# A two-layer block on one core: bodies of the mixer written out for all batches, with the jobs of all five engines in another order

## The reference

```python
h = _layernorm(x) * (1 + ca) + sa
# linear attention, 16 heads of 16
qf, kf = elu(h @ wq.T) + 1, elu(h @ wk.T) + 1
kv = einsum('bhsd,bhse->bhde', kf, h @ wv.T)
x = x + ga * ((qf @ kv) / (qf . sum(kf) + EPS) @ wo.T + bo)
h = _layernorm(x) * (1 + cb) + sb
# softmax attention, 16 query heads, 4 key and value heads, 512 x 512 scores for each head
scores = einsum('bhqd,bhkd->bhqk', q, k) / sqrt(16)
src = h + softmax(scores) @ v @ ow + ob
src = _rmsnorm(src, norm1_w)
src = src + _moe(src, gate_w, w1, w2)     # sigmoid router, top 2 of 8 experts, capacity
x = x + gb * _rmsnorm(src, norm2_w)
```

## Time and profile before

| engine | busy us | share of the span | instructions |
|---|---|---|---|
| PE | 3107.1 | 92% | 18289 |
| DVE | 2105.6 | 63% | 5860 |
| ACT | 1634.8 | 49% | 3647 |
| POOL | 1203.8 | 36% | 1507 |

### The profile page before, as it was taken

How to read it: one execution, slowest core, us unless ns; L and a number is a source line. 1 busy time by engine, 2 the same in 40 slices (tenths; PEclk the granted TensorE clock), 3 DMA queues, 4 the chain that set the end, 5 groups by cost and what they waited for, 6 DMA issues and landing times. The chain is left out here.

```text
span 3365.7 us, 58089 instructions
## 1 busy us (share of the span) xinstructions
PE 3107.1 (92%) x18289; PEld 1914.7 (57%) x18289; DVE 2105.6 (63%) x5860; ACT 1634.8 (49%) x3647; POOL 1203.8 (36%) x1507
## 2 busy tenths in 40 slices
PE   6899999999989977999999999999999859999995
PEld 3667767677665653344444444444444338888882
DVE  7777777777772235677777777777777632222225
ACT  3565565655641113666666666666666521111113
POOL 2132232322342123334444444444443234444445
PEclk9999999999999988999999999999999979999998
DMA  8010100101025851112222222222222128888866
GB/s 265 5 48 24 41 30 24 47 24 40 32 70 195 300 187 35 51 54 72 74 74 74 74 69 73 72 72 68 73 69 75 52 75 216 215 219 217 219 187 200
DMA packets 269091, 337.44 MB, mean 100 GB/s; under 512 B 43679, under 2 KB 218386, under 8 KB 268832
## 3 DMA queue, kind: packets, MB, share of 16 engines
q1 hardware_dynamic: 239840, 296.62, 28.3%
q0 software_dynamic: 28464, 34.71, 4.8%
q10 hardware_dynamic: 544, 3.15, 0.2%
HBM read 225.77 MB, written 113.95 MB: 101 GB/s over the span
## 5 line engine op out<-in xcount | busy, mean ns | idle before, releaser
L2426 ACT ACTIVATE pT<-psum 128x512 f32<-128x512 f32 x1024 | 599.2, 599 | 362.5 <-PE psum L3204 343.6
L2720 DVE TENSOR_REDUCE negmax<-psum 128x2 f32<-128x1024 f32 x512 | 624.6, 1221 | 199.1 <-PE psum L3174 182.0
L3204 PE MATMUL psum<-q_stack,k_stack 99*128 99x512 bf16 x1024 | 379.3, 384 | 20.8 <-issue 10.5
L3174 PE MATMUL psum<-k_stack,q_stack 96*128 96x512 bf16 x1024 | 312.2, 387 | 47.0 <-DVE negmax L2720 37.3
L3535 POOL DMA_INDIRECT src_rows<-ye,place x142 | 222.7, 1568 | 317.3 <-DVE place L3571 140.1
L939 ACT ACTIVATE probs<-probs,negmax 128x256 f32<-128x256 f32 x512 | 252.8, 495 | 137.7 <-DVE negmax L1031 134.0
L3548 ACT ACTIVATE actT_x<-psum 128x512 f32<-128x512 f32 x142 | 84.8, 597 | 439.6 <-PE psum L3624 429.4
L3587 DVE TENSOR_SCALAR ye<-psum,weight 128x256 f32<-128x256 f32 x142 | 62.2, 480 | 361.4 <-PE psum L3636 361.3
L3218 PE MATMUL psum<-pT,v_tile 128*32 128x512 f32 x2048 | 275.0, 609 | 1.0 <-ACT pT L2426 1.0
L3624 PE MATMUL psum<-xT_x,w_x 128*128 128x256 f32 x1136 | 258.5, 381 | 0.0
L3636 PE MATMUL psum<-w_x,actT_x 128*128 128x256 f32 x1136 | 256.6, 379 | 0.0
(11 more groups left out here) (392 smaller groups left out, 5805.3 us busy)
## 6 DMA issues: line engine op xcount, KB each, us to landing
w_x<-in_L_ffn_w_dram SPq DMA_DIRECT2D x142, 512.0 KB, 4.6
w_e<-in_L_ffn_w_dram SPq DMA_DIRECT2D x46, 1024.0 KB, 6.8
q_stacks<-q_part SPq DMA_DIRECT2D x192, 128.0 KB
q_stack<-q_stacks SPq DMA_DIRECT2D x64, 384.0 KB, 3.6
padded<-w_e SPq DMA_DIRECT2D x32, 650.0 KB, 6.0
xe<-padded SPq DMA_DIRECT2D x71, 260.0 KB
gate_rows<-mods SPq DMA_DIRECT2D x66, 256.0 KB, 3.4
x<-in_L_attn_x_dram SPq DMA_DIRECT2D x16, 512.0 KB, 8.7
```

Of the source, the lines that this page charges most:

```text
L2426: act.activation(pT[:, 4 * (s % 2) + r, :], bank(m, 2 + n % 2), ACT.Exp, scale=float(DHQ) ** -0.5)\
L2720: dve.tensor_reduce(negmax[:, p // 2, h:h + 2], m.psum[:, at:at + 2, :], AX.X, ALU.max, negate=True)\
L3174: mm = pe.matmul(bank(m, at + j), q_stack[0:K_SCORE, h, t * P:(t + 1) * P], k_stack[0:K_SCORE, g, :], start=True, stop=True)
L3204: pe.matmul(bank(m, 2 + n % 2), k_stack[:, g, kc * P:(kc + 1) * P], q_stack[:, REP * g + r, :], start=True, stop=True).then_inc(sT_done, 1)
```

## The change

The job functions stay as they are, but for one thing: the three Newton steps on VectorE get scratch tiles of their own, which lets two of them stand next to each other. The bodies lose their loop over steps, the hardware loop goes, and every engine has its jobs written out in another order. Body -1 becomes `entry()`, with the same jobs in the same order. Every job of every batch is there as often as before. The line numbers of the jobs on TensorE grow by 144, those on GpSimd by 2.

```diff
-            for b in range(-3, 2):
+            for b in range(-3, -1):
                 body(b, b % 2, lambda k: 0 <= b + k < B)
-            with loop(nc, pe, 0, 2) as i:
-                for u in range(4):
-                    body(4 * i + (u + 2), u % 2, lambda k: True)
-            for b in range(10, B + 3):
+            entry()
+            for b in range(0, B + 3):
                 body(b, b % 2, lambda k: 0 <= b + k < B)
...
-            def newton(step, out, var, eps, last):
-                h = m.newton[:, 0:NT]
+            def newton(step, h, out, var, eps, last):
...
-                newton(step, rstd1[:, :], mv1[:, :, 1], LN_EPS, stats1)
+                newton(step, m.newton[:, 0:NT], rstd1[:, :], mv1[:, :, 1], LN_EPS, stats1)
...
-                newton(step, rstd2[:, par, :], mv2[:, par, :, 1], LN_EPS, rstd2_ready)
+                newton(step, m.newton[:, NT:2 * NT], rstd2[:, par, :], mv2[:, par, :, 1], LN_EPS, rstd2_ready)
...
-                newton(step, rstdr[:, :], mvr[:, :, 1], EPS_NORM, rstdr_ready)
+                newton(step, m.var_eps[:, 0:NT], rstdr[:, :], mvr[:, :, 1], EPS_NORM, rstdr_ready)
```

```diff
                     max_rows(b + 1, 0)
-                if part(1):
-                    load_h2_rows(b + 1)
-                if part(1):
-                    store_second(b + 1)
-                if part(3):
-                    load_rows(b + 3)
-                if part(1):
-                    load_stack(b + 1, 2)
-                if part(-1):
-                    store_src(b - 1, 1 - par)
-                if part(1):
-                    load_stack(b + 1, 3)
-                if part(1):
-                    max_rows(b + 1, 1)
+                    store_second(b + 1)
+                    load_stack(b + 1, 2)
+                    load_stack(b + 1, 3)
+                    max_rows(b + 1, 1)
+                if part(-1):
+                    store_src(b - 1, 1 - par)
+                if part(1):
+                    load_h2_rows(b + 1)
+                if part(3):
+                    load_rows(b + 3)
```

VectorE and ScalarE, one place each of the new bodies (ScalarE's `second_part(b + 1, 2)` stood at step 13, between two `exps` of that step):

```diff
+                if part(1):
+                    row_max(b + 1, 1, 0)
+                if part(-1):
+                    choose_top(b - 1)
+                if part(1):
+                    row_max(b + 1, 1, 1)
+                    row_max(b + 1, 1, 2)
+                if part(2):
+                    gate(b + 2, 0)
+                if part(-1):
+                    choose_index(b - 1)
+                if part(1):
+                    row_max(b + 1, 1, 3)
...
+                if part(1):
+                    copy_max(b + 1, 0)
+                if part(2):
+                    copy_o1T(b + 2, 1)
+                if part(1):
+                    second_part(b + 1, 2)
```

More of the change, by code:

```diff
@@ L3413, in _ @@
-            for b in range(-3, 2):
+                if part(0):
+                    scoresT(b, 0, 0)
+                if is_entry(b - 1):
+                    project1(1, 0)
+                    project1(1, 1)
+                if part(0):
+                    max_scores(b, 1, 4)
+                    scoresT(b, 0, 1)
+                if part(2):
+                    transpose_hidden(b + 2, 0)
+                if part(0):
+                    scoresT(b, 0, 2)
+                if part(-1):
+                    weigh(b - 1, 15, 1 - par)
@@ new lines, in body @@
+                if part(1):
+                    transpose_hidden2(b + 1, 1)
+                if part(0):
+                    weigh(b, 3, par)
+                    max_scores(b, 2, 4)
+                if part(-1):
+                    transpose_weighed(b - 1, 3)
+                if part(1):
+                    queries_keys(b + 1, 0)
+                if part(0):
+                    max_scores(b, 2, 5)
+                    scoresT(b, 4, 2)
+                    scoresT(b, 4, 3)
+                if part(2):
+                    keys_values(b + 2, 1)
@@ new lines, in body @@
+                if part(2):
+                    keys_values(b + 2, 3)
+                if part(0):
+                    scoresT(b, 9, 2)
+                    max_scores(b, 3, 7)
+                    scoresT(b, 9, 3)
+                    weigh(b, 8, par)
+                    scoresT(b, 10, 0)
+                if part(1):
+                    max_scores(b + 1, 0, 0)
+                if part(0):
+                    scoresT(b, 10, 1)
+                    weigh(b, 9, par)
+                    transpose_max(b, 3)
+                    scoresT(b, 10, 2)
@@ new lines, in body @@
+                if part(0):
+                    scoresT(b, 15, 0)
+                if part(1):
+                    max_scores(b + 1, 1, 1)
+                if part(0):
+                    scoresT(b, 15, 1)
+                if part(2):
+                    project1(b + 2, 0)
+                if part(1):
+                    max_scores(b + 1, 1, 2)
+                if part(0):
+                    scoresT(b, 15, 2)
+                    scoresT(b, 15, 3)
+                if part(1):
+                    values(b + 1)
@@ L3414, in _ @@
+                if part(0):
+                    weigh(b, 14, par)
+                if part(1):
+                    max_scores(b + 1, 1, 3)
+                if part(2):
+                    project1(b + 2, 1)
+            for b in range(-3, -1):
                 body(b, b % 2, lambda k: 0 <= b + k < B)
-            with loop(nc, pe, 0, 2) as i:
-                for u in range(4):
-                    body(4 * i + (u + 2), u % 2, lambda k: True)
-            for b in range(10, B + 3):
+            entry()
```

934 lines of the change are left out of this document (577 added, 357 removed).

## The result

The changed kernel takes 3394.22 us (median of 4 runs, 3387.26 to 3410.70), beside 3367.11 for the kernel before. The ratio is 1.0084, with a 95% interval of 1.0066 to 1.0102: 0.8% slower, where 1% faster was forecast. The profiled execution of the changed kernel took 3387.26 us, the shortest of the four; its span is 3385.5.

What follows compares the result with a forecast made beforehand. TensorE (PE), 95% busy, was taken to bound the mixer, so only its standing time could be won: -1.3 - 0.4 - 0.7 - 0.5 + 0.5 - 0.3 = -2.7 us a body, 13 bodies, -35 us: 3333 us, range 3305 to 3371.

Steps and rivals of the forecast that it cites:

- GpSimd and SyncE: `last_part(b + 1, 2)` ends 2 to 3 us later, but `store_second` does not move; costed at nothing.
- rival 3: Slower: GpSimd's chain ends 6 us later than forecast, TensorE waits 4 us a body; +17, 3385 us; chance 0.11.
- the same sum: `cut_max(b + 1, 0)` and `choose_top` lie under GpSimd's resid work instead of its xn work, at the same price.
- Place A: First pairs of the next batch: 1.98 us of waits go, 0.3 left, 0.4 new stack-transfer wait; 1.3 us less a body.
- rival 1: Transfers decide Place A: it gives 0.3 us instead of 1.3; -22, 3346 us; chance 0.20.
- Place B: End of the body: 1.0 us goes, 0.2 stays, 0.4 new at pair (1, 4) of the next; 0.4 us less.
- Places C and D: Behind `keys_values(b + 2, 2)`, 0.7 us less a body; at `queries_keys(b + 1, 0)`, 0.5 us less.
- Elsewhere: New waits at `max_scores(b, 3, 1)`, (3, 5) and `project2(b - 1, 1)`: +0.5 us a body; small old waits go: -0.3.
- The loop: Writing out bodies 2 to 9 is worth 0 to 6 us, mostly counted in place C already; taken as 0.
- Rival 2: The waits only move and VectorE keeps bodies at 87 us: 3368 us, at most 5 either way; chance 0.14.

Runs made afterwards that it cites:

- the kernel of 3326.8: The changed kernel with GpSimd's whole body in the order of before and `place(b - 2)` in its early spot on VectorE: 3326.82 us, ratio 0.9894.
- the kernel with both moves undone: The changed kernel with `place(b - 2)` back early on VectorE, `add_bias` and `normalise_first` back on GpSimd: 3349.85 us, ratio 0.9949.
- the mirror: The kernel before, loop and other engines' orders kept, with GpSimd's body alone in the changed order: 3415.72 us, ratio 1.0150.

## Why the prediction was wrong, step by step

**The step that failed** is the one on GpSimd and SyncE, "so nothing moves ... I cost this at nothing". It looked at GpSimd's new order only for when its own results are ready (rival 3), and not for what VectorE does meanwhile. It should have read +35 us (with `place` early) to +57.5 us (with it late), over 13 bodies 2.7 to 4.4 us each. Neither `place`, moved from behind (b, 2, 5) to behind (b, 3, 0), nor `scale_src` has a term in the forecast at all, though in the old trace GpSimd was idle beside both: at `place` in a wait of 26.85 us that ScalarE's q_part ended, at `scale_src` in its wait for src ("4.09 <-DVE src L2793"). That idle time was the cover, and the change filled it. What the runs showed in place of the nothing: `over` and the copy longer by 3.4 us a body together, `scale_src` by 3.1, and PE's waits behind them of 2.9 to 3.1 and 1.9 us.

**The rule was cited and then confined.** The Trainium skill ("SBUF — State Buffer", Who interferes with whom) says that a VectorE instruction with two SBUF inputs contends with a GpSimd instruction that reads SBUF, that a copy, cast or tensor_scalar in a two-port mode and a GpSimd instruction block each other fully, that the order of issue decides who blocks, and that `tensor_reduce` never contends. By that rule, the traces agree: 166 to 2393 ns for the copy, 478 to 1249 for `scale_src`, 1221 to 1219 for the reduction. The forecast applied it to `cut_max` and `choose_top` alone and concluded "the same sum". Each of the other moved jobs had to be held against GpSimd's new neighbours.

**What held.** In a body of the changed kernel (body 8) PE's waits of 0.15 us or more are: 0.44, 2.87, 0.23, 0.37 and 1.88. Without the two large ones that is 1.04, where body 8 of before has 3.35.
- Place A: the wait of 0.63 is gone, the second stays, 0.37 for 0.39; no wait for a k_stack DMA appears, so the 0.4 taken for it was wrong, and rival 1 with it.
- Place B: the 0.82 is gone, and a new wait of 0.44 stands exactly at (b + 1, 1, 4), behind `choose_index` and the reduction of (1, 3); 0.4 was taken.
- Places C and D: the third product waits no more (0.59 before), nor does `queries_keys` (0.36). The 0.44 of the prediction was a mean with one wait of 1.51 in it.
- Elsewhere: 0.5 was added for three new waits. In body 1, which nothing hides, PE has only two waits of 0.15 us or more, 0.44 at place B and 0.23 at (b + 1, 0, 4); none of the three named is there.
- The sum of these, -2.7 us a body, fits where nothing hides it: body 1 fell by 3.3 us, and the kernel of 3326.8 lies 31.8 below the one that is only written out, for 35 forecast. That difference has the same GpSimd order on both sides.
- The loop: 0 was taken, 0 to 6 allowed, 7.8 measured. "Most of that difference is place C" was wrong: written out without a job moved, place C's wait stays, and only its excess in looped bodies goes.

**Of the rivals**, the third had the sign and its engine, and even its price (3385 for 3394), but not its mechanism: it named GpSimd held up by VectorE and late stacks, and it was VectorE held up by GpSimd, with no wait for a stack. That its price came so near is luck. Rival 2 (the waits only move) is out. Neither forecast nor rivals had a term for the clock, since it read 1.00 throughout; a third of the loss is there.

**Open.** Which waits are followed by a slow stretch and which are not is not settled. In the kernel of 3326.8, eight of eleven waits of 1.27 us were followed by slow matmuls and three were not; in the kernel with both moves undone, none of eleven such waits was; and in the kernel before, four waits of 1.44 to 1.51 us were not. Nor is it settled why `over` was held through five additions, while in the mirror's block (1939.26 to 1943.39, six additions in a row) VectorE's instructions take 0.51 to 0.78 us each, about one addition apiece. The share of SyncE's order was never undone alone.

## What to carry to other kernels

An idle stretch of GpSimd beside small VectorE instructions on SBUF may be what keeps them small: before moving work into it, list what VectorE runs there, and price each SBUF-to-SBUF instruction between one addition (0.7 us here) and the whole block that could lie beside it (3.35 us here). The victim need not be heavy: two instructions of 0.16 us, longer by 3.4 together, cost a body more than all the well-placed moves gave it. When PE is 95% busy at full clock, allow for a second price behind each new wait: matmuls at half speed, which came behind some waits and not behind others of the same length. And try undoing the side engine's order before doubting the main one's.

## What the runs showed of the hardware that was not expected

- VectorE was held for more than one GpSimd instruction: `over` began 0.02 us behind the first of six additions and got through only at about the end of the fifth (3.35 us), the copy behind it at the end of the sixth. Other blocks without a gap let VectorE's instructions through after about one addition each, so what decides is open.
- Which small instruction is hit is a matter of tenths of a us: `over` or the copy (means of 1323 and 2393 ns), `slot_k` in another order (3047), newton steps in a third (647), always beside GpSimd's additions.
- In one kernel eight of eleven waits of 1.27 us of a PE that is busy otherwise were followed by matmuls at half speed, up to 3.66 us for four instead of 1.96, and a body longer by 1.65 us; in another none of eleven was. The record of the granted clock shows such a stretch some 10 us after the slow matmuls: the first slow pair (1.04 us) starts at 1644.29, the drop is recorded at 1654.2. Look for it by durations.
